# Moving row statistics, masked reciprocals and an input split to other turns in a cross attention loop

## What is computed

```
x = x + xattn(layernorm(x), ctx, mask, mask, Wq, bq, Wk, bk, Wv, bv)   # x: 16 x 256 channels x 512
q = Wq target + bq;  k = Wk source + bk;  v = Wv source + bv           # 16 heads of 16
dot = q^T k / 4;  mask = tmask[t] * smask[s]
dot = mask * dot - (1 - mask) * 1e6
out = (softmax(dot) * mask) v
```

## Time and profile before

| | |
|---|---|
| median of 3 executions | 3043.39 us (3041.3 to 3044.64) |
| the profiled execution | 3046.28 us, span 3044.8 us, mean granted PE clock 0.944 |
| cross attention in it | about 1420 to 2420 us of the span |
| 1500 to 2300 us: busy | PE 703.6, DVE 667.0, ACT 555.2, POOL 449.8 of 800 us |
| 1500 to 2300 us: granted PE clock, DMA share | 0.97, 0.72 |

### The profile page before, as it was taken

The page is one execution under the profiler, slowest core; times in us unless marked ns, Lnnn a source line. Parts: engine busy times, 40 slices in busy tenths (PEclk is TensorE's granted clock), DMA queues, the critical chain, the costliest instruction groups (busy, mean ns, idle before and its releaser), DMA issues. The chain is left out here.

```text
span 3044.8 us, 49987 instructions
## 1 busy us (share of the span) xinstructions
PE 2656.2 (87%) x15042; PEld 1824.1 (60%) x15043; DVE 1936.9 (64%) x3971; ACT 1354.3 (44%) x2725; POOL 1041.6 (34%) x1209
## 2 busy tenths in 40 slices
PE   7999999999999999994788888988888533299997
PEld 6888888888888888882333333333333122166665
DVE  6555566656555566653788888888888368444443
ACT  4333344444333344431476667667767422122221
POOL 2111122221111122211355556556546346423322
PEclk9999999999999999996799999999999866599999
DMA  3111011122110011102767677677777364455554
GB/s 111 42 41 41 1 41 41 41 83 70 42 42 31 10 41 41 41 28 58 133 116 134 123 132 130 127 137 137 132 133 121 60 222 162 160 100 98 103 102 78
DMA packets 140496, 265.50 MB, mean 87 GB/s; under 512 B 39168, under 2 KB 42112, under 8 KB 138896
## 3 DMA queue, kind: packets, MB, share of 16 engines
q1 hardware_dynamic: 111712, 195.58, 28.9%
q0 software_dynamic: 24496, 60.72, 9.6%
q10 hardware_dynamic: 4224, 8.39, 0.7%
HBM read 139.43 MB, written 64.90 MB: 67 GB/s over the span
## 5 line engine op out<-in xcount | busy, mean ns | idle before, releaser
L1397 DVE TENSOR_REDUCE b_negmax<-b_ps_s 128x2 f32<-128x1024 f32 x512 | 616.6, 1221 | 121.6 <-PE b_ps_s L1533 117.4
L1272 ACT ACTIVATE b_probs<-b_ps_s 128x1024 f32<-128x1024 f32 x512 | 517.1, 1022 | 258.8 <-PE b_ps_s L1544 258.0
L255 POOL TENSOR_SCALAR probs<-probs,rinv 128x256 f32<-128x256 f32 x256 | 242.6, 948 | 1099.2 <-DVE rinv L407 1099.2
L289 ACT ACTIVATE probs<-ps_s,negmax 128x128 f32<-128x128 f32 x256 | 94.2, 368 | 480.8 <-DVE negmax L400 480.8
L1544 PE MATMUL b_ps_s<-b_stack 56*128 56x512 f32 x1024 | 253.5, 493 | 50.4 <-DVE b_negmax L1397 33.6
L1544 PEld LDWEIGHTS b_ps_s<-b_stack 56*128 56x128 f32 x1024 | 97.2, 187 | 333.2 <-issue 181.1
L1533 PE MATMUL b_ps_s<-b_stack 54*128 54x512 f32 x1024 | 230.0, 446 | 67.7 <-ACT b_probs L1272 49.7
L1555 PE MATMUL b_ps_o<-b_probs,b_v_stack 128*32 128x512 f32 x2048 | 282.6, 625 | 5.9 <-ACT b_probs L1272 5.9
L511 PE MATMUL ps_proj<-xT_h,wq_h 128*128 128x512 f32 x512 | 215.7, 421 | 0.0
L2150 POOL DMA_INDIRECT out<-e_y,e_place_int x71 | 110.8, 1561 | 276.4 <-DVE e_y L2213 147.0
L511 PE MATMUL ps_proj<-xT_h,wq_l 128*128 128x512 f32 x512 | 201.2, 393 | 0.0
(11 more groups left out here) (278 smaller groups left out, 6757.3 us busy)
## 6 DMA issues: line engine op xcount, KB each, us to landing
b_stack<-b_split SPq DMA_DIRECT2D x240, 128.0 KB
e_row<-rows_by_expert SPq DMA_DIRECT2D x71, 258.0 KB, 3.2
x_in<-in_x SPq DMA_DIRECT2D x16, 1024.0 KB, 7.5
x<-acc SPq DMA_DIRECT2D x16, 1024.0 KB, 5.1
b_out_tiles<-row_sum_inverses SPq DMA_DIRECT2D x64, 256.0 KB
b_stack<-b_late SPq DMA_DIRECT2D x96, 128.0 KB
acc<-in_x SPq DMA_DIRECT2D x8, 1024.0 KB, 5.8
acc<-x SPq DMA_DIRECT2D x8, 1024.0 KB, 5.8
```

Source lines behind the costliest of these rows:

```text
L255: nc.gpsimd.tensor_scalar(probs[:, s, P:3 * P], probs[:, s, P:3 * P], rinv[:, s, 1:2], None, ALU.mult).then_inc(probs_done, 1)
L289: nc.scalar.activation(probs[:, s, 0:P], ps_s[s][:, 0:P], ACT.Exp, bias=negmax[:, s, 0:1], accum_out=rowsum[:, s, 0:1])
L1272: nc.scalar.activation(probs[:, k % 2, p, :, :], ps[:], ACT.Exp, scale=0.25).then_inc(e_done, 1)
L1397: nc.vector.tensor_reduce(negmax[:, k, p, :], ps[:], AX.X, ALU.max, negate=True).then_inc(m_reduced, 1)
```

## The change

The computation is the same. On DVE the row statistics of sequence b+2 go from the end of turn (1, 3) to the end of (2, 0), and every masked reciprocal from the end of its quad's last turn, k = 3, to the end of k = 2. On POOL `norm_scale(b + 2)` goes ahead of residual 3, store and load. On ACT the two halves of the normalisation go to (2, 2) and (3, 1), where both stood at (3, 1), and the high part goes from behind both exponentials of (3, 2) to between the two of (3, 3). SP's and PE's orders stay.

```diff
+        STATS_AT, RECIPROCALS_AT = (2, 0), 2
@@ POOL
+                    if not tail:
+                        norm_scale(b + 2)
                     if not first:
                         residual(b - 1, g - 1, 3)
                         wait_alone(pool, y_done, g + QUADS, (consts, 5))
                         store_y(b - 1)
                         load_res(b)
-                    if not tail:
-                        norm_scale(b + 2)
@@ ACT
+                def normalised_part(b, k):
+                    if k == 0:
+                        act.wait_ge(scale_done, b + 1)
+                        if not (static(b) and b == 0):
+                            act.wait_ge(xs_low, b)
+                    nc.scalar.activation(xn[:, k, :], x_in[:, k, :], ACT.Identity, bias=shift[:, k:k + 1],
+                                         scale=rstd[:, k:k + 1]).then_inc(xn_done, 1)
...
                             output(g + q - 1, (q - 1) % QUADS)
+                        if (q, k) == (3, 3) and not tail:
+                            x_high(b + 2)
                         exps(where, b, q, k, 1)
...
                         if not tail:
+                            if (q, k) == (2, 2):
+                                normalised_part(b + 2, 0)
                             if (q, k) == (2, 3):
                                 context_high(b + 2)
                             if (q, k) == (3, 1):
-                                normalised(b + 2)
-                            if (q, k) == (3, 2):
-                                x_high(b + 2)
+                                normalised_part(b + 2, 1)
@@ DVE
-                        if (q, k) == (1, 3) and not tail:
+                        if (q, k) == STATS_AT and not tail:
                             normalise(b + 2)
-                        if k == TBL - 1 and not (first and q == 0):
+                        if k == RECIPROCALS_AT and not (first and q == 0):
                             masked_reciprocal(g + q - 1, b + (q - 1) // QUADS, (q - 1) % QUADS)
```

More of the change, by code:

```diff
@@ L1239, in normalised @@
                 def normalised(b):
-                    act.wait_ge(scale_done, b + 1)
-                    if not (static(b) and b == 0):
-                        act.wait_ge(xs_low, b)
                     for k in range(CT):
-                        nc.scalar.activation(xn[:, k, :], x_in[:, k, :], ACT.Identity, bias=shift[:, k:k + 1],
-                                             scale=rstd[:, k:k + 1]).then_inc(xn_done, 1)
+                        normalised_part(b, k)
+                def normalised_part(b, k):
[5 more added lines that the diff above has]
+                                         scale=rstd[:, k:k + 1]).then_inc(xn_done, 1)
                 def x_high(b):
```

## The result

| | before | after |
|---|---|---|
| median of 9 executions, same chip | 3041.3 us (3036.93 to 3046.19) | 3051.62 us (3047.81 to 3060.3) |
| ratio after/before | | 1.0035, 95% interval 1.0023 to 1.0048 |
| profiled execution, span, mean granted PE clock | 3046.28, 3044.8, 0.944 | 3059.26, 3057.8, 0.934 |

The change made the kernel slower by 10 us. The forecast of 3057 is 5 us off, its sign is right, and 3051.62 lies in the range. Whether it was right for its reasons is the question of the rest.

The account below looks back on a forecast made before the run. PE, busy for 87% of the span, was taken as the bound. Terms 7.5 + 23 - 6.5 - 4 - 6 = +14 us took the profiled 3046.28 to 3060.3, the median to 3057 us; 80% range 3030 to 3085.

Parts of the forecast that it names:

- The wait for the sums: DVE's reciprocal in quad 1, at k = 2, waits 2.6 us for row sums; bounds 0.5 and 4 us.
- Its cost without the clock: PE's max_scores(2, 0, 0) waits 1.25 us for DVE; +0.5 us in each of 15 sequences, +7.5 us.
- Clock falls: PE's clock falls behind two waits at the start of quad 2 in 13 of 15 sequences: +23 us (0 to +37).
- rival without falls: PE stays at 2.4 GHz behind the new wait at the start of quad 2; 3034 us, chance 0.17.
- Statistics: DVE's statistics, moved to (2, 0), stand beside turns that are PE's: nothing more; up to 0.5 us without a projection there.
- ACT: Normalisation and copy leave busy places in quad 3, so PE's two waits shrink: -0.3 us x 14 = -4 us (0 to -8).
- POOL: Residual 3 and eight DMAs behind it start 1.2 us late, but the sequence is about as much later: priced at nothing.
- The turn of the sequence: x_low on POOL and DVE's split collide less at the sequence's end: -6 us, between -24 and +10.
- The sum: All terms together: 7.5 + 23 - 6.5 - 4 - 6 = +14 us, where -6.5 takes off today's three clock falls.
- The waiting step: The +7.5 and +23 us for PE's wait and clock at quad 2's start, less 6.5 for today's falls.
- two rivals on the faster side: No clock falls at quad 2's start: 3034 us, chance 0.17; quad 1's sums there in time: 3018 us, chance 0.08.
- late POOL: Rival: late x-row load makes residual 0 and x_low end in the split, 18 us more: 3075 us, chance 0.17.

Follow-up runs that it names:

- filler run: Changed kernel plus five unread matmuls on PE between the first exp_scores of (2, 0) and the max_scores behind it: 3032.91 us, ratio 0.9969 against before.
- run with all reciprocals back: Changed kernel with all reciprocals back at k = 3: 3039.05 us, ratio 0.9979 against before.
- statistics and norm: Kernel before with only DVE's statistics moved to (2, 0) and norm_scale ahead of residual 3 on POOL: 3036.34 us, ratio 0.9978.
- sums first: Changed kernel with SP's copy of quad 0's row sums ahead of the three half-stack DMAs in quad 1's list: 3039.03 us, ratio 0.9978 against before.

## Why the prediction was right, point by point

- **The wait for the sums.** Right. Forecast 2.6 us; measured about 3.1 (3.20 in b = 4, where they came at 1749.8, 5.2 us after SP sent for them; the forecast had 4.1). `max_scores(2, 0, 0)` waits 1.84 us on the mean where 1.25 were worked out, as the longer first wait asks.
- **Its cost without the clock.** +7.5 forecast. With the falls gone (filler run) quads 1 and 2 take 29.65 us against 29.35 before, whose three falls make 6.5 / 14 = 0.46 of that. The filler run still has one fall, 2.6 us of quad 2 or 0.19 a sequence. So 0.57 x 14 = 8 us, as forecast.
- **Clock falls.** +23 forecast with 13 of 15; 14 of 15 came, and the filler run, which takes 13 of them away, prices them at 22 us by the quads and 20 by the ratio, 1.7 us each. This is the part that decided the sign, and the rival without falls is refuted; its 3034 us is what the filler run gives, 0.9969 x 3041.3 = 3032. The working to the +23 was less sound than its result: 1.3 and 3.0 less 0.5 make 1.65 on the mean and not 1.75, and the 1.7 us of slack in it come from no row. Nor does the size of the second wait decide alone, as the three falls before seemed to say: the clock fell behind second waits of 0.35, 0.46 and 0.72 us in the run with all reciprocals back, and did not behind one of 0.74 in that with statistics and norm, nor behind three of 1.35 to 1.44 with the sums first. The Trainium skill (TensorE: Matmul & The Clock Gate, HAM oscillation — how this bites in real kernels) lets the clock fall on a long gap. Here short waits are enough: it falls behind two, of 0.88 and 1.35 to 2.5 us with one pair of matmuls between them.
- **Statistics.** Priced at nothing beside the wait, which hides what they free. By themselves they are worth 1 us a sequence (quad 2 from 15.67 to 14.68). So the change held a gain that its reciprocals covered, and the forecast's sum was right only for the two together.
- **ACT.** -4 forecast. Quad 3 lost 0.15 us on the mean, 2 us in all, and 0.4 by its median. With the high part alone moved it lost 0.19. What the sum did not have is that the later copy keeps `x_low` off the product at (3, 2): with the reciprocals alone quad 3 takes 14.63 us, in the changed kernel 12.60, which is 28 us in 14.
- **POOL.** Nothing forecast, on the ground that the sequence is as much later. Nothing was lost, and the load is issued 12.8 us behind the split of quad 1 on the mean, 13.5 before. But that this cover is what counts is not borne out: with the sums first, quad 1 is short and the load is still never waited for. The waits of 25 to 35 us came in the versions that also have POOL's new order and the reciprocal of quad 1 at k = 3, and go with a slowest transfer of 12.7 to 13.9 us. Right in the number, then, and by luck in its ground.
- **The turn of the sequence.** This step failed. Forecast -6 for the wrong reason, that DVE would wait for sums at (3, 2) too. It hardly did: SP had waited 98 us for reciprocals before and waits 10 now, and is early enough there. Measured -19 us, near the bound of -24, through the load of x rows, whose slowest transfer fell from 12.3 to 7.2 us. The forecast read the casts and the load's wait as two things, and priced them apart. The load decides where `x_low` and so the cast stand: a quarter of what was there was taken where it was nearly all. It also had no term for the clock falls behind the turn, which came with 11 of the 19 us. Why the load lands sooner stays open; it goes with SP's earlier reading of the inverses.
- **The sum.** Forecast +14. By quads, 28 - 2 - 19 is +7 (+6 between the first and last splits, 865.0 to 870.7 us); by the medians +10. The waiting step was 4 us too low and the turn 13 too high. The two errors partly met.

The two rivals on the faster side and the late POOL are out: the sums are not in time, the falls are there, and POOL never waits for its load.

## What to carry to other kernels

Before an operation that waits for a DMA is moved to an earlier turn, look where its transfer stands in the issuing queue, because it is the send, and not the need, that sets the landing; here four places looked alike and two of them had slack. With those two moved, beside the rest of the change, the kernel is 18 us faster than before, with all four 10 us slower. Price a short wait of TensorE with what the clock does behind it, above all where a second wait follows closely, and try a few useless matmuls in the gap: that run takes clock and wait apart. And when a load stops or starts being late, compare its issue, its landing and its neighbours in the queues before blaming the time it had: here the issue stood still and the landing moved by 5 us.

## What the runs showed of the hardware

- With DVE's wait left as it was, filling part of PE's idle time of 1.35 to 2.5 us with 1.4 us of matmuls took away 13 of 14 clock falls, though 0.88 and 0.71 us of waiting were left. The falls cost 1.6 us a sequence.
- The cast of the maxima on DVE (128x16) takes 0.18 us alone and, where it meets POOL's two-input subtraction of `x_low`, lasts until that ends: 0.85 us where POOL is 1.6 us ahead, 2.35 at most. DVE's own two-input operations do the same: the product behind the reciprocal (128x16) took 2.42 instead of 0.18 at most. Beside POOL's scaling of the values by a column (128x64, one tensor) the cast took 0.18. Reducing maxima out of PSUM was not held up: 1.22 us on the mean in the changed kernel, beside POOL's two-input operations or not.
- A load of the same four times 128 KB, in b = 4, took between 4.9 and 6.9 us from issue to landing in the changed kernel, and between 5.9 and 12.8 in that with reciprocals early in quads 0 and 2, at a DMA share of 0.73 to 0.74 in both profiles' long stretch. It goes with how far ahead another queue sent for 256 KB; no run took that apart.
